# Two-layer conditioned transformer on one core: transposes of the probabilities in front of the slot's score matmul

## The reference, cut to what matters

```python
x = _L0_cond_ref(x, itok_B_0_15, ...)         # adapter 256 -> 64 -> 256 by an expert per batch, GELU, LayerNorm
# L1: x is (8, 512, 256)
x = _ln(src) * (1.0 + scale) + shift          # modulated by a timestep embedding
q, k, v = (x @ Wq + bq), (x @ Wk + bk), (x @ Wv + bv)      # split into 16 heads
scores = einsum('bhqd,bhkd->bhqk', q / sqrt(HEAD_DIM), k) + attention_bias
scores = where(src_mask, -inf, scores)
probs = softmax(scores, axis=-1)
ctx = einsum('bhqk,bhkd->bhqd', probs, v)
x = x + (ctx @ Wo + bo)
h = _ln(x) * g2 + beta2
return x + _gelu2(h @ W1 + b1) @ W2 + b2      # F = 1024, _gelu2(x) = x * sigmoid(1.702 x)
```

## Time and profile before

| | us |
|---|---|
| median of 3 runs | 940.47 |
| lowest, highest | 938.56, 943.39 |
| profiled execution: time | 938.38 |
| profiled execution: span from first to last instruction | 936.5 |

### The profile page before, as it was taken

How to read it: one execution, slowest core, us unless ns; L and a number is a source line. 1 busy time by engine, 2 the same in 40 slices (tenths; PEclk the granted TensorE clock), 3 DMA queues, 4 the chain that set the end, 5 groups by cost and what they waited for, 6 DMA issues and landing times.

```text
span 936.5 us, 20734 instructions
## 1 busy us (share of the span) xinstructions
PE 884.3 (94%) x6476; PEld 662.1 (71%) x6476; DVE 703.0 (75%) x1905; ACT 704.8 (75%) x1670; POOL 705.8 (75%) x412
## 2 busy tenths in 40 slices
PE   5668799999999999999999999999999999999988
PEld 2445566777777777777777777787777777777766
DVE  6657778878788886878687887888778787675652
ACT  2547788878797787879797787878788787867651
POOL 3746988988787976988687986979788887877700
PEclk7978999999999999999999999999999999999999
DMA  6689979766987679776997769776897769766300
GB/s 187 196 265 314 301 214 269 239 213 197 278 264 222 212 217 294 230 216 209 256 286 226 211 211 279 227 238 202 253 272 209 216 192 264 240 209 182 124 2 23
DMA packets 147967, 207.41 MB, mean 221 GB/s; under 512 B 14409, under 2 KB 62346, under 8 KB 147858
## 3 DMA queue, kind: packets, MB, share of 16 engines
q1 hardware_dynamic: 145474, 204.10, 73.3%
q10 hardware_dynamic: 2384, 1.97, 0.7%
HBM read 185.03 MB, written 20.99 MB: 220 GB/s over the span
## 4 chain that ended last, share of the span: by engine, by line
PE 82%; issue 6%; POOL 5%; DVE 3%; ACT 2%; DMA 1%; SPq 0%; DVEq 0%; POOLq 0%; ACTq 0%
PE tp L904 20%; PE la L824 11%; PE pv L862 11%; PE sc L897 11%; PE lc L809 11%; PE lb L641 5%; POOL bias_s L523 4%; PE lb L843 3%; PE lb L657 2%; PE la L631 1%; DVE xm L1231 1%; PE lc L623 1%; PE la L614 1%; ACT bias_s L1103 1%; PE lb L614 1%
## 5 line engine op out<-in xcount | busy, mean ns | idle before, releaser
L523 POOL TENSOR_TENSOR bias_s<-mask_f,bias_s 128x1024 f32<-128x1024 f32 x256 | 601.2, 2370 | 128.4 <-DMA bias_s<-in_bias 127.6
L1535 DVE CUSTOM_DVE_ANT_0 bias_s<-sc,bias_s 128x512 f32<-128x512 f32 x512 | 347.9, 684 | 166.7 <-PE sc L897 162.5
L1103 ACT ACTIVATE bias_s<-bias_s,mx 128x512 f32<-128x512 f32 x512 | 371.2, 725 | 79.5 <-DVE mx L1535 77.2
L904 PE MATMUL tp<-ident,bias_s 128*128 128x128 f32 x2048 | 310.1, 274 | 7.2 <-ACT pT L1109 3.7
L904 PEld LDWEIGHTS tp<-ident,bias_s 128*128 128x128 f32 x2048 | 252.6, 141 | 86.6 <-issue 17.1
L1109 ACT COPY pT<-tp 128x512 f32<-128x512 f32 x335 | 195.2, 583 | 96.1 <-PE tp L904 93.6
L897 PE MATMUL sc<-stk,stq 128*128 128x512 bf16 x512 | 196.2, 384 | 20.3 <-DVE mx L1535 14.7
L862 PE MATMUL pv<-pT,v_all 128*32 128x256 f32 x2048 | 124.5, 384 | 0.0
L824 PE MATMUL la<-w_s,act_s 128*128 128x256 f32 x496 | 124.3, 380 | 0.0
L1542 DVE COPY pT<-tp 128x512 f32<-128x512 f32 x177 | 121.2, 685 | 1.9 <-PE tp L904 1.8
L809 PE MATMUL lc<-hT,w_s 128*128 128x256 f32 x464 | 119.4, 380 | 2.5 <-ACT hT L1058 1.9
(11 more groups left out here) (209 smaller groups left out, 812.1 us busy)
## 6 DMA issues: line engine op xcount, KB each, us to landing
bias_s<-in_bias SPq DMA_DIRECT2D x256, 512.0 KB, 4.7
stk<-k_parts SPq DMA_DIRECT2D x128, 96.0 KB, 3.9
stq<-q_parts SPq DMA_DIRECT2D x126, 96.0 KB, 4.1
k_parts<-kb SPq DMA_DIRECT2D x32, 192.0 KB, 2.3
q_parts<-qb SPq DMA_DIRECT2D x30, 192.0 KB, 2.4
xT<-in_x_t SPq DMA_DIRECT2D x8, 512.0 KB, 7.7
k_parts<-kb SPq DMA_DIRECT2D x32, 128.0 KB, 2.4
stk<-k_parts SPq DMA_DIRECT2D x64, 64.0 KB, 4.4
```

Source lines behind the costliest of these rows:

```text
L523: pool.tensor_tensor(tile, mask_f[:, :, :], tile, ALU.subtract).then_inc(s["masked"], 1)
L904: last = pe.transpose(tp[n % 2][:, kt * P:(kt + 1) * P], bias_s[:, n // 2 % NB, n % 2, kt * P:(kt + 1) * P], ident[:, :])
L1103: act.activation(tile, tile, ACT.Exp, bias=mx[:, t:t + 1], scale=-1.0, accum_out=sums[:, j, head_of(hh):head_of(hh) + 1]).then_inc(s["prob ...
L1535: dve.tensor_tensor_reduce(out=tile, in0=sc[t % 2][:, :], in1=tile, scale=1.0, scalar=BIG, op0=ALU.add, op1=ALU.min, accum_out=mx[:, t:t + ...
```

## The change

In PE's queue the two places of each slot are exchanged. Before, a slot held its score and then the transposes of the tile three slots back. Now it holds the transposes and then the score. The work at .0, .3 and .6 keeps its positions, so what stood between score and transposes (.3) now stands between transposes and score. The other engines' queues, the tables, the lag of three slots and the waits are as before.

```diff
                 for t in range(TI):
-                    each_slot(i, t, steps, lambda: score(t) if attn else None,
-                              lambda: turn(TI * i + t - LAG) if (attn if t >= LAG else prev) else None)
+                    each_slot(i, t, steps, lambda: turn(TI * i + t - LAG) if (attn if t >= LAG else prev) else None,
+                              lambda: score(t) if attn else None)
```

## The result

| | before | after |
|---|---|---|
| median, us (4 runs each) | 940.1 | 967.7 |
| lowest, highest | 938.56, 943.39 | 963.72, 968.31 |
| profiled execution: time | 938.38 | 963.72 |
| profiled execution: span | 936.5 | 961.9 |

The ratio is 1.028, 95% interval 1.0241 to 1.0319: the changed kernel is 2.8% slower. The forecast was 964.0, with a range of 946 to 976.

The account below looks back on a forecast made before the run. PE, busy for 94% of the span, was taken to bound the kernel. Terms 9.8 + 7.0 + 5.5 + 1.2 + 0 = 23.5 us on the profiled 938.38 gave 961.9, plus 2.1 to the median 964.0; range 946 to 976.

Parts of the forecast that it names:

- PE saturated, waits are lost time: Iterations 2 to 13: PE is always at work (52.63 of 53 us), so every wait on it is lost for good.
- Place 1: Slots 6 to 13: score 6 comes 0.70 later, making max 9 and L614 as late; 14 x 0.70 = 9.8 us.
- Place 2: Slots 14 to 17: transposes wait for DVE's copies of tiles 11 and 12, 0.27 each; 13 x 0.54 = 7.0 us.
- Place 3: End of iterations with a Gelu: transposes 29 wait for ACT's late copy of tile 27; 5 x 1.1 = 5.5 us.
- Small terms: Weight loads behind P·V 1.7, score 0's saved wait -1.4, i = 15 and the end 0.9; sum 1.2 us.
- The start: Iterations 0 and 1: transposes filling waits, -3.4, against new waits, +3.6; taken as 0 us.
- The sum: Whole kernel: 9.8 + 7.0 + 5.5 + 1.2 + 0 = 23.5 us more, giving 964.0.
- A sign that failed: Page after: PE's busy time the same within 3 us, and about 51.3 to 51.9 in a middle stretch of 53 us.
- C: Whole kernel: no change, PE's spare time absorbs the waits; 940 to 943 us, chance 0.08.
- B: Slots 7, 8, 25 and 29 run dry as well, four waits of 0.25; +14 on top, 978 us, chance 0.13.
- A: Only slots 6 to 13 cost, and only their transposes; 14 x 0.43 = 6.0, 946.5 us, chance 0.09.

Follow-up runs that it names:

- The filler: The kernel before with the fifth pair of L809 matmuls at 12.6 in place of 13.0, ahead of L614: 933.1 us, ratio 0.9923.
- the part stood alone: The kernel before with transposes first in slots 6 to 10 only, the score first in all others: 946.4 us, ratio 1.0073.
- the experiment: The changed kernel with the score first again in slots 30, 31 and 0: 958.8 us, ratio 1.0186.

## Why the prediction was right, step by step

- **PE saturated, waits are lost time.** Right. The filler gave back all of the 0.51, and the sum of the waits makes the time.
- **Place 1, 0.70 for an iteration.** The mechanism was right, the size too large. The place measured 0.53 by the starts (0.42 of it in slots 12 and 13), and 0.52 where the part stood alone. I took max 9 to be late by all that score 6 was. Score 6 was late by 0.71, but from max 6 to max 9 DVE took 4.66 in place of 4.77: 0.1 of slack that I had read as work without a gap. ACT and the gate had a little too: from max 9 to xm are 2.66 us (338.08 to 340.74) in place of 2.74 (330.61 to 333.35). I also named one feeder; score 2, by way of exp 4 and the gate, is a second. It adds nothing in the changed kernel, but holds DVE once score 6 is in time.
- **Place 2, 0.54.** 0.27 and 0.26 measured, 0.27 and 0.27 forecast; 0.63 came back with the load behind P·V and small gaps in the same slots.
- **Place 3, 1.1 behind each Gelu.** 1.03 measured, 1.05 by the experiment.
- **Small terms.** Behind each P·V 0.05 or 0.06 are lost (332.15 to 332.64 for four transposes in place of 0.44), 0.04 forecast; that this is the weight load is my reading of its place. The Trainium skill, "TensorE: Matmul & The Clock Gate", section "LDWEIGHTS (loading the stationary operand)", lets only columns count, which would make it nothing; the loads measured 98 and 141 ns for 128 columns each, so the rows decide. The end cost 4.6 from i = 13 on; my terms for it make about 4.
- **The start, 0.** Left open: its profiles differ by 7 us with one and the same order, and I have no run that says what makes them differ. So neither the 3.4 of waits that the transposes were to fill nor the 3.6 against them is shown; the profiles of the two kernels differ by 2.7.
- **The sum.** Eleven iterations lie between the two L631: 18.1 measured, and by my terms some 19, too much for place 1. The span grew by 25.4, 23.5 forecast, since the start and the end gave more. That the total came so near is in part luck: place 1 was too large by 0.17 in each of 14 iterations, 2.4 us, and the 2.7 of the start, which I had put at nothing, made up for it. The median lies 4.0 above the profiled execution, where I had added 2.1.
- **A sign that failed.** PE's busy time was to stay within 3 us and rose by 10.3; and the stretches of 53 us read 51.10 and 51.97, just outside the 51.3 to 51.9 that I named. I had seen that a modelled end covers 0.16 of a wait, but not that every new wait therefore adds up to 0.16 to the busy time.
- **Rivals.** C (absorbed) falls by the stretches, and with it the reading of weight loads as the measure of free time (the Trainium skill, "Perfetto Trace Analysis", section "Identifying the Most-Contended Engine"): in the kernel before with L809 at 12.6, PEld was at 77% (40.94 of 53 us) when PE had nothing to spare. B (slots 7, 8, 25 and 29 run dry as well) shows no gap over 0.06 us. A gave only the transposes' time at one place; three places ran dry.

## What to carry to other kernels

In a schedule written by hand, moving an instruction by half a slot shortens the slack of two edges at once: from its input, and from the release of the buffer that it writes. Find the engine that is saturated, list for each of its instructions the slack of both, and look where nothing but short instructions follow one another. When the buffer was the short edge, a longer lag gave nothing here (983.2 us for 967.7, with the list of copies left as it was); other work in front of the waiting instruction gave back the wait, and work behind it gave nothing for that wait.

## What was not expected of the hardware

A matmul's modelled end hides 0.16 us of each wait behind it: 0.88 by the starts is 0.72 on the row, 1.03 is 0.87. The 0.27 and 0.26 us ahead of 349.00 and 350.81 have no mark at all, and count as 0.11 and 0.10 of idle time in the busy share. Waits under 0.16, such as the 0.05 behind P·V, are hidden whole. In an iteration without a Gelu the loss is 1.20, of which PE's busy time shows 0.66 (52.63 to 51.97 in 53 us). The other 0.54 is booked as busy time; over fourteen iterations that is at least 7.6 of the 10.3 us by which PE's busy time rose. Only the differences of starts show all of it.

The start of the program, up to the L631 of i = 2, took from 155.6 to 162.3 us in profiles of one order, while the middle repeats to 0.1 us.
